# One to four matmuls into unused halves of three PSUM banks, ahead of each tile's product in a gather loop

## The chip, the cores and the metric

The kernel runs on one core of one Trainium2 chip. The metric is the time on the device in microseconds (us), from one launch; smaller is better. The core has the engines TensorE (PE; its weight loads stand in a row of their own, PEld), VectorE (DVE), ScalarE (ACT), GpSimd (POOL) and SyncE (SP), which run side by side and wait for each other by semaphores.

## The reference

The program is one layer of a graph network. The part around the change is the message passing, `agg[dst] += weight * xn[src]` over 100,000 edges and 6,250 nodes of width 256, followed by a linear layer. Beside it run a linear attention and, later, a mixture of eight experts.

```python
def _L0_gnn_ref(x, edge_row, edge_col, edge_val, W, b):
    gathered = edge_val[:, None] * x[edge_col]
    agg = jax.ops.segment_sum(gathered, edge_row, num_segments=N_NODES)
    return jnp.einsum('nd,od->no', agg, W) + b
...
xn = _layernorm(x, axis=-1)
x = x + _L0_gnn_ref(xn, src, dst, edge_weight, L0_gnn_W, L0_gnn_b) + _L0_mix_ref(xn[None], ...)[0]
x = x + _L0_ffn_ref(_layernorm(x, axis=-1)[None], ...)[0]
```

## The kernel before

The edges have been sorted beforehand into tiles of 128 that all end in the same block of 128 nodes; there are 902 such tiles. The linear layer is applied first, so that `z_d` in HBM holds one row per node: a high half and a low half, each 256 numbers of 16 bits. The function `graph` then does five things for each tile t, each on an engine of its own:

- POOL (`gather`, L961) starts an indirect DMA that fetches the 128 rows of `z_d` which the tile's edges name (1 KB each) into one of 12 row buffers (`rows[k]`, k = t mod 12, `UG` = 12). It waits first until the product of 12 tiles earlier is finished (`s_mm[k]`), because that product read the buffer.
- DVE (`compare`, L1067) builds a 0/1 matrix that says which edge goes to which node, six tiles ahead (`LEAD`).
- ACT (`weigh`, L985, twice) multiplies it by the high and the low half of the edge weights into one of eight matrices `hot` (`HG` = 8).
- PE (`product`, L1286 to L1288) multiplies it with the rows in three matmuls of 256 columns, all into columns 0 to 255 of one of three PSUM banks (`out_ps`, `BG` = 3). It waits for `hot`, for the row DMA (`s_row[k]`) and for the add of three tiles earlier (`s_add`), which frees the bank. The last of the three matmuls raises `s_mm[k]`.
- DVE (L1206) waits for `s_mm[k]`, adds the bank to the block of `acc` to which the tile belongs, and raises `s_add[k]`.

Each engine runs its own instructions in the order in which they are written. A turn of the loop (`turn`) does 24 tiles. There are 38 turns, the last of 14 tiles, and other work is written between the tiles: in turns 0 to 12 (312 tiles, called stage 1 here) the keys and values of the attention (`features`), in turns 13 to 26 (336 tiles, stage 2) its queries and output (`attention`), and in turns 27 to 37 (254 tiles, stage 3) in part the splitting of the experts' weights, which needs no PE. The PE work of stages 1 and 2 is in 32-bit numbers (L1222, L1230, L1235, L1257 and so on). `B0` = 13 and `L0` = 27 are the turns at which stages 2 and 3 begin. The gather loop lies between 326 and 1681 us of the span. Before it the edges are sorted, and after it come routing and experts.

Of the kernel before, what the change touches and what calls it, by code (L numbers as in the profile page):

```python
# [11 lines left out]
N, D = 6250, 256  # L12
# [12 lines left out]
UG, HG, OG, BG, LEAD = 12, 8, 4, 3, 6  # L25
# [40 lines left out]
def matrix(a, n, m):  # L66
    return a.rearrange("p (n m) -> p n m", n=n, m=m)
# [30 lines left out]
def build(nc, A, out):  # L98
    ctx = ExitStack()
    with ctx:  # L100
# [38 lines left out]
        with nc.cleanup_on_exit():  # L139
            collect(nc, c)  # L140
        graph(nc, c, A)
        route(nc, c, A)
        experts(nc, c, A)
# [646 lines left out]
def graph(nc, c, A):  # L790
# [8 lines left out]
    hot = [matrix((misc if k < 5 else more).take(2 * P, F16), 2, P) for k in range(HG)]  # L799
# [17 lines left out]
    den, a = big.take(NE), big.take(D)  # L817
# [7 lines left out]
    turns, LOOPS, B0, L0, L1 = ET // UG, ET // (2 * UG), 13, 27, 32  # L825
# [1 line left out]
    assert UG < tiles_of(LOOPS - 1)  # L827
    M2, M9, LAST = 8, 16, 25
    assert 4 * B0 >= NT + 3 and 4 * (L0 - B0) >= NT + 5 and L1 + 5 <= LOOPS and 24 * L1 >= 3 * CW // 2
    out_ps = [c.bank[k][:, 0:D] for k in range(BG)]  # L830
    ctx_ps, tr_ps = matrix(c.bank[3][:, 0:DH * (P + 1)], DH, P + 1), c.bank[3][:, 0:D]
    k_ps, q_ps = [c.bank[4 + u][:, 0:D] for u in range(2)], [matrix(c.bank[4 + u][:, 0:D], DH, P) for u in range(2)]
    v_ps, pj_ps = c.bank[6][:, 0:D], c.bank[7][:, 0:D]
# [5 lines left out]
    s_row, s_mm, s_add = ([S(f"{name}{k}") for k in range(UG)] for name in ("row", "mm", "add"))  # L839
# [15 lines left out]
    def wait(e, sem, n):  # L855

        if not (isinstance(n, int) and n <= 0):
            e.wait_ge(sem, n)
# [25 lines left out]
    with nc.Block(no_gpsimd_drain=True) as block:  # L884
# [331 lines left out]
        def _(e):  # L1216
            def features(j, h, k, s):
                if k == 0 and live(s - 2):
                    e.wait_ge(s_kf, s - 1)
                    e.wait_ge(s_vo, s - 1)  # L1220
                    for m in range(DH):
                        l = e.matmul(ctx_ps[:, m, :], kf[h % 2][:, m * P:m * P + P], vo[h % 2][:, m, :], start=False, stop=False)  # L1222
                    l.then_inc(s_ctx, 1)
                    if isinstance(s, int) and s - 2 == NT - 1:
                        e.matmul(ctx_ps, zeros[:, 0:P], matrix(zeros[:, 0:DH * (P + 1)], DH, P + 1), start=False, stop=True).then_inc(s_ctx, 1)
                if k == 1 and live(s):
                    e.wait_ge(s_x[h], 16 * (j + 1))
                    wait(e, s_kf, s - 1)
                    for x in range(DH):
                        l = e.matmul(k_ps[h % 2], xT[h][:, x, :], wk[:, x, :], start=x == 0, stop=x == 1)  # L1230
                    l.then_inc(s_k, 1)
                if k == 3 and live(s):
                    wait(e, s_vo, s)
                    for x in range(DH):
                        l = e.matmul(v_ps, xT[h][:, x, :], wv[:, x, :], start=x == 0, stop=x == 1)  # L1235
                    l.then_inc(s_vz, 1)

            def attention(j, h, k, b):
                if k == 0 and live(b - 2):
                    if isinstance(b, int) and b == 2:  # L1240
                        e.wait_ge(s_bd, 1)
                    e.wait_ge(s_qf, b - 1)
                    wait(e, s_at, b - 2)
                    for m in range(DH):
                        l = e.matmul(nd_ps[:, m, :], qf[h % 2][:, m, :], sums[:, m, :], start=True, stop=True)
                    l.then_inc(s_nd, 1)
                if k == 1 and live(b):
                    e.wait_ge(s_x[h], 16 * (j - B0 + NT // 4 + (2 if h == 0 else 1)))
                    if isinstance(b, int) and b == 0:
                        e.wait_ge(s_w2, 32)  # L1250
                    if isinstance(b, int) and b < 2:
                        e.wait_ge(s_kf, NT)
                    else:
                        e.wait_ge(s_qf, b - 1)
                    for m in range(DH):
                        for x in range(DH):
                            l = e.matmul(q_ps[h % 2][:, m, :], wq[:, x, m * P:m * P + P], xT[h][:, x, :], start=x == 0, stop=x == 1)  # L1257
                    l.then_inc(s_q, 1)
                if k == 3 and live(b - 2):
                    e.wait_ge(s_at, b - 1)  # L1260
                    wait(e, s_aT, b - 2)
                    for m in range(DH):
                        l = e.transpose(tr_ps[:, m * P:m * P + P], a[:, m * P:m * P + P], c.ident)
                    l.then_inc(s_tr, 1)
                if k == 5 and live(b - 3):
                    e.wait_ge(s_aT, b - 2)
                    wait(e, s_mix, b - 3)
                    for m in range(DH):
                        l = e.matmul(pj_ps, aT[:, m, :], wp[:, m, :], start=m == 0, stop=m == DH - 1)
                    l.then_inc(s_pj, 1)  # L1270

            def scales(h, k):
                if k == 3 and h == 2:
                    e.wait_ge(s_bmax, 1)
                    e.transpose(most_ps[0:2, 0:P], most2[:, 0:2], c.ident).then_inc(s_mt, 1)
                if k == 3 and h == 3:
                    e.wait_ge(s_mr, 1)
                    e.matmul(most_ps[:, 256:260], ones[0:2, :], both[0:2, :], start=True, stop=True).then_inc(s_mb, 1)

            def product(j, t):  # L1280
                q, k = j * 2 + t // UG, t % UG
                e.wait_ge(s_hot, 2 * (j * 2 * UG + t + 1))
                e.wait_ge(s_row[k], 16 * (q + 1))
                wait(e, s_add[(k - BG) % UG], j * 2 + (t - BG) // UG + 1)
                o, w = out_ps[t % BG], hot[t % HG]
                e.matmul(o, w[:, 0, :], rows[k][:, 0:D], start=True, stop=False)  # L1286
                e.matmul(o, w[:, 0, :], rows[k][:, D:2 * D], start=False, stop=False)  # L1287
                e.matmul(o, w[:, 1, :], rows[k][:, 0:D], start=False, stop=True).then_inc(s_mm[k], 1)  # L1288

            def turn(j, at):  # L1290
                for t in range(tiles_of(at)):
                    h = t // 6
                    if at < B0:
                        features(j, h, t % 6, j * 4 + h)
                    elif at < L0:
                        attention(j, h, t % 6, (j - B0) * 4 + h)
                        if at == LAST:
                            scales(h, t % 6)
                    product(j, t)
            e.wait_ge(s_ones, 4)  # L1300
            e.wait_ge(s_w, 16 * 4)
            e.matmul(bias_ps, ones[0:2, :], bias[0:2, :], start=True, stop=True).then_inc(s_bias, 1)
            e.matmul(ctx_ps, zeros[:, 0:P], matrix(zeros[:, 0:DH * (P + 1)], DH, P + 1), start=True, stop=False)
            loops(e, turn)


# [597 lines left out]
```

## Time and profile before

| | |
|---|---|
| median of 3 runs | 2469.26 us (2467.01 to 2470.97) |
| profiled execution, its own time | 2453.38 us |
| its span, first to last instruction | 2451.7 us |
| mean granted TensorE clock, share of full speed | 0.82 |
| PE busy, PE weight loads busy | 1685.1 us (69%), 1215.1 us (50%) |
| DVE, ACT, POOL busy | 1447.4, 1306.2, 1409.0 us |

The page also gives the span in 40 slices of 61 us: a digit is a tenth of the slice, for the engines as busy time and for PEclk as the clock that was granted to TensorE. The gather loop takes slices 6 to 27 or so. A PE at 2.4 GHz all the time would show 9 there. Idle time before an instruction is put down in the views to what ended it. "remote" stands for a semaphore whose raising the profile can't connect with the end of an instruction, and "issue" for nothing that the profile shows.

### The profile page before, as it was taken

How to read it: one execution, taken by the hardware profiler on the slowest of the kernel's cores; microseconds unless marked ns; L12 is line 12 of the kernel's file. 1: busy time of each engine (PE TensorE's matmuls, PEld its weight loads, DVE VectorE, ACT ScalarE, POOL GpSimd, SP SyncE). 2: the span in 40 equal slices, each digit the busy share in tenths (PEclk: the TensorE clock that was granted, in tenths of full speed). 3: DMA queues.
4: the chain of work that ended last, by engine and by line, in shares of the span. 5: the costliest groups of instructions: out<-in, count | busy, mean ns of one | idle time of the engine just before them, and what ended most of it. 6: DMA issues, size and time to landing. Idle time of an engine off the chain costs nothing. (4 is left out here: it accounts for less than half of the span.)

```text
span 2451.7 us, 53365 instructions
## 1 busy us (share of the span) xinstructions
PE 1685.1 (69%) x13546; PEld 1215.1 (50%) x13546; DVE 1447.4 (59%) x3501; ACT 1306.2 (53%) x4202; POOL 1409.0 (57%) x1346
## 2 busy tenths in 40 slices
PE   6776446666666566666664444445379999999998
PEld 3465424444444455555542122213277777777776
DVE  7997535555555565555555555557755555555555
ACT  6454345555555455555555655655306666666665
POOL 3688846666666666666666666665354444444443
PEclk8998768888887787787886565655569999999999
DMA  4022144444444443333333334434302222222222
GB/s 144 18 84 70 54 137 131 131 132 131 129 129 129 132 116 100 100 101 99 100 90 90 91 107 122 151 115 142 109 29 45 47 47 45 47 47 48 46 47 31
DMA packets 140235, 224.43 MB, mean 92 GB/s; under 512 B 34055, under 2 KB 94673, under 8 KB 139955
## 3 DMA queue, kind: packets, MB, share of 16 engines
q0 software_dynamic: 67040, 146.22, 23.2%
q1 hardware_dynamic: 73042, 76.15, 10.2%
q8 instruction: 99, 1.62, 0.3%
q14 instruction: 54, 0.43, 0.1%
HBM read 181.40 MB, written 41.82 MB: 91 GB/s over the span
## 5 line engine op out<-in xcount | busy, mean ns | idle before, releaser
L961 POOL DMA_INDIRECT misc<-z_d,consts x902 | 858.1, 951 | 509.7 <-issue 252.3
L1206 DVE SCALAR_TENSOR_TENSOR acc<-ps,consts,acc 128x256 f32 x902 | 434.3, 482 | 535.7 <-remote 461.1
L1286 PE MATMUL ps<-misc 128*128 128x256 f16 x565 | 186.3, 330 | 309.3 <-DVE acc L1206 150.9
L985 ACT ACTIVATE rec<-rec,misc 128x128 f16<-128x128 f16 x674 | 228.8, 392 | 199.0 <-DVE rec L1067 124.8
L1742 ACT ACTIVATE misc<-ps,misc 128x128 f32<-128x128 f32 x840 | 240.1, 368 | 170.7 <-PE ps L1709 155.4
L1709 PE MATMUL ps<-misc,big 128*128 128x128 f16 x1680 | 327.4, 220 | 0.0
L1707 PE MATMUL ps<-misc,big 128*128 128x128 f16 x1680 | 327.1, 220 | 0.1
L1708 PE MATMUL ps<-misc,big 128*128 128x128 f16 x1680 | 326.9, 220 | 0.0
L1723 PE MATMUL ps<-big,rec 128*128 x840 | 320.2, 382 | 7.3 <-DVE rec L1843 4.9
L985 ACT ACTIVATE misc<-rec,misc 128x128 f16<-128x128 f16 x678 | 228.4, 391 | 145.3 <-DVE rec L1067 114.4
L1775 POOL DMA_INDIRECT misc<-tok_d,pos x105 | 103.8, 988 | 304.0 <-ACT misc L1813 240.5
L1286 PEld LDWEIGHTS ps<-misc 128*128 128x128 f16 x565 | 60.7, 107 | 413.1 <-issue 318.0
L1067 DVE TENSOR_SCALAR rec<-consts,misc 128x128 f16<-128x128 f16 x676 | 186.6, 276 | 59.5 <-issue 57.1
L1841 DVE CAST rec<-misc 128x512 f16<-128x512 f32 x210 | 89.8, 427 | 219.3 <-ACT misc L1742 212.5
L985 ACT ACTIVATE misc<-misc 128x128 f16<-128x128 f16 x452 | 155.9, 392 | 114.4 <-DVE misc L1067 91.9
L1286 PE MATMUL ps<-misc,rec 128*128 128x256 f16 x337 | 112.6, 334 | 141.8 <-issue 78.3
L1707 PEld LDWEIGHTS ps<-misc,big 128*128 x1680 | 164.8, 98 | 88.0 <-issue 1.2
L1782 POOL DMA_INDIRECT out<-misc,pos x105 | 170.5, 1624 | 53.4 <-issue 32.2
L1725 PE MATMUL ps<-big,rec 128*128 x735 | 200.4, 273 | 0.0
L1287 PE MATMUL ps<-misc 128*128 128x256 f16 x565 | 191.5, 339 | 0.0
L1288 PE MATMUL ps<-misc 128*128 128x256 f16 x565 | 191.0, 338 | 0.0
L369 POOL DMA_INDIRECT rec_d<-misc x112 | 155.0, 1384 | 50.1 <-issue 33.8
(335 smaller groups left out, 3884.0 us busy)
## 6 DMA issues: line engine op xcount, KB each, us to landing
big<-in_w2T SPq DMA_DIRECT2D x60, 256.0 KB
misc<-z_d,consts POOLq DMA_INDIRECT x902
big<-xT_d SPq DMA_DIRECT2D x98, 128.0 KB
big<-in_w1T SPq DMA_DIRECT2D x32, 256.0 KB
tok_d<-misc SPq DMA_DIRECT2D x50, 132.0 KB, 1.9
xT_d<-misc SPq DMA_DIRECT2D x49, 128.0 KB
z_d<-misc SPq DMA_DIRECT2D x49, 128.0 KB
acc<-in_x SPq DMA_DIRECT2D x1, 6144.0 KB
```

The lines of the kernel that those rows point to most:

```text
L961: e.indirect_dma_start(out=rows[k], out_offset=None, in_=c.z_d, in_offset=bass.IndirectOffsetOnAxis(ap=idx[u][:, k:k + 1], axis=0)).then_i ...
L985: e.activation(hot[t % HG][:, half, :], same[t % OG], ACT.Copy, scale=near[t // UG][:, t % UG, 1 + half:2 + half]).then_inc(s_hot, 1)
L1206: e.scalar_tensor_tensor(out=rows_of, in0=out_ps[t % BG], scalar=c.gain, in1=rows_of, op0=ALU.mult, op1=ALU.add).then_inc(s_add[k], 1)
L1286: e.matmul(o, w[:, 0, :], rows[k][:, 0:D], start=True, stop=False)
L1287: e.matmul(o, w[:, 0, :], rows[k][:, D:2 * D], start=False, stop=False)
L1288: e.matmul(o, w[:, 1, :], rows[k][:, 0:D], start=False, stop=True).then_inc(s_mm[k], 1)
L1707: e.matmul(o, w1h[:, at], xT[s.u][:, h, :], start=h == 0, stop=False)
L1708: e.matmul(o, w1h[:, at], xT[s.u][:, DH + h, :], start=False, stop=False)
L1709: l = e.matmul(o, w1l[:, at], xT[s.u][:, h, :], start=False, stop=h == DH - 1)
L1723: l = e.matmul(y_ps[s.u], high[s.u][:, m, :], c.w2[:, bass.ds(at, 2 * D)], start=m == 0, stop=m == HB - 1)
L1725: e.matmul(y_ps[s.u][:, 0:D], low[s.u][:, m, :], c.w2[:, bass.ds(at, D)], start=False, stop=False)
L1742: l = e.activation(hidden[:, m, :], h_ps[s.u][:, m, :], ACT.Relu, bias=b1x[s.u][:, m:m + 1])
```

## The change

Each tile's product gets extra matmuls ahead of it: two in stage 1, one in stage 2, four in stage 3. They use the tile's own high `hot` matrix as weights and both halves of `hot` as 256 moving columns. They write columns 256 to 511 of the tile's own bank, which nothing reads. The wait for the bank (`s_add`) is moved ahead of the wait for the rows, and the new matmuls stand between the two. They raise no semaphore. In all they are 2 x 312 + 1 x 336 + 4 x 254 = 1976 matmuls with as many weight loads. No instruction of DVE, ACT, POOL or SP is added or moved.

```diff
-    out_ps = [c.bank[k][:, 0:D] for k in range(BG)]
+    out_ps, unused_ps = ([c.bank[k][:, half * D:half * D + D] for k in range(BG)] for half in range(2))
...
-            def product(j, t):
+            def product(j, t, steady):
                 q, k = j * 2 + t // UG, t % UG
+                o, w = out_ps[t % BG], hot[t % HG]
                 e.wait_ge(s_hot, 2 * (j * 2 * UG + t + 1))
+                wait(e, s_add[(k - BG) % UG], j * 2 + (t - BG) // UG + 1)
+                for _ in range(steady):
+                    e.matmul(unused_ps[t % BG], w[:, 0, :], w.rearrange("p a n -> p (a n)"), start=True, stop=True)
                 e.wait_ge(s_row[k], 16 * (q + 1))
-                wait(e, s_add[(k - BG) % UG], j * 2 + (t - BG) // UG + 1)
-                o, w = out_ps[t % BG], hot[t % HG]
                 e.matmul(o, w[:, 0, :], rows[k][:, 0:D], start=True, stop=False)
...
-                    product(j, t)
+                    product(j, t, 2 if at < B0 else 1 if at < L0 else 4)
```

On PE at the first tiles of stage 1, the difference reads as follows. `ps` is a PSUM bank, `misc` holds `hot` and `rows`, and `big` holds the operands of the attention; x2 are two instructions alike.

```order
-L1302 MATMUL ps<-big 128x256
-L1303 MATMUL ps<-big 128x258
-L1286 MATMUL ps<-misc 128x256
-L1287 MATMUL ps<-misc 128x256
-L1288 MATMUL ps<-misc 128x256
+L1304 MATMUL ps<-big 128x256
+L1305 MATMUL ps<-big 128x258
+L1286 MATMUL ps<-misc 128x256 x2
+L1288 MATMUL ps<-misc 128x256
+L1289 MATMUL ps<-misc 128x256
+L1290 MATMUL ps<-misc 128x256
 L1230 MATMUL ps<-big 128x256 x2
```

Two matmuls now precede the three of the product (which move down by two lines), and the key matmuls of `features` (L1230) follow as they did.

On PE at the first tiles of stage 3, two tiles of before and two of the change:

```order
-L1286 MATMUL ps<-misc 128x256
-L1287 MATMUL ps<-misc 128x256
-L1288 MATMUL ps<-misc 128x256
-L1282 ISA
-L1286 MATMUL ps<-misc 128x256
-L1287 MATMUL ps<-misc 128x256
-L1288 MATMUL ps<-misc 128x256
```

```order
+L1286 MATMUL ps<-misc 128x256 x4
+L1287 ISA
+L1288 MATMUL ps<-misc 128x256
+L1289 MATMUL ps<-misc 128x256
+L1290 MATMUL ps<-misc 128x256
+L1283 ISA
+L1286 MATMUL ps<-misc 128x256 x4
+L1288 MATMUL ps<-misc 128x256
+L1289 MATMUL ps<-misc 128x256
+L1290 MATMUL ps<-misc 128x256
```

A tile of stage 3 has seven matmuls of 256 columns on PE where it had three (ISA rows are waits and register work).

## Rows read from the trace of the kernel before

**Rows 1.** The page, costliest groups: busy and mean ns, then idle before and its releaser.

```profile
L961 POOL DMA_INDIRECT misc<-z_d,consts x902 | 858.1, 951 | 509.7 <-issue 252.3
L1206 DVE SCALAR_TENSOR_TENSOR acc<-ps,consts,acc 128x256 f32 x902 | 434.3, 482 | 535.7 <-remote 461.1
```

**Rows 2.** Windows, one per stage: length, busy us (xcount) by engine, PEclk, DMA, GB/s.

```profile
360.00:794.00 434.00, 275.38 (x1435) 190.08 (x1434) 243.00 (x723) 234.22 (x771) 273.43 (x290) 0.84 0.44 130
794.00:1302.00 508.00, 320.55 (x1902) 246.92 (x1900) 291.02 (x952) 268.91 (x880) 318.75 (x337) 0.82 0.36 104
1302.00:1673.00 371.00, 168.41 (x747) 73.86 (x747) 197.65 (x563) 201.86 (x603) 242.16 (x253) 0.59 0.38 112
```

**Rows 3.** Line L961 from 360 to 1673 us: idle us before it, times, by releaser.

```profile
  issue: 226.3, 713
  remote: 224.7, 138
  PE ps L1288: 27.4, 24
```

**Rows 4.** Timeline of POOL, stage 1: the gathers around one stall.

```profile
746.84 0.94 POOL L961 DMA_INDIRECT misc<-z_d,consts  x1 [0.30 <-issue]
748.08 0.94 POOL L961 DMA_INDIRECT misc<-z_d,consts  x1 [0.30 <-issue]
749.33 0.95 POOL L961 DMA_INDIRECT misc<-z_d,consts  x1 [0.30 <-issue]
752.06 0.94 POOL L961 DMA_INDIRECT misc<-z_d,consts  x1 [1.78 <-remote]
```

**Rows 5.** Timeline of PE, the same stretch.

```profile
745.19 0.27 PE L1286 MATMUL ps<-misc,rec 128*128 128x256 f16 x1
745.29 0.27 PE L1287 MATMUL ps<-misc,rec 128*128 128x256 f16 x1
745.40 0.27 PE L1288 MATMUL ps<-misc,rec 128*128 128x256 f16 x1
...
747.67 0.27 PE L1288 MATMUL ps<-misc 128*128 128x256 f16 x1
752.62 0.37 PE L1286 MATMUL ps<-misc 128*128 128x256 f16 x1 [4.68 <-issue]
```

**Rows 6.** Timeline of DVE, the same stretch.

```profile
746.65 0.25 DVE L1067 TENSOR_SCALAR rec<-consts,misc 128x128 f16<-128x128 f16 x1
751.99 0.48 DVE L1206 SCALAR_TENSOR_TENSOR acc<-ps,consts,acc 128x256 f32 x1 [5.09 <-remote]
...
752.61 0.48 DVE L1206 SCALAR_TENSOR_TENSOR acc<-ps,consts,acc 128x256 f32 x1
```

**Rows 7.** DMA from 747 to 753 us, in 40 slices of 0.15 us.

```profile
GB/s 164 55 137 273 164 246 0 0 0 109 218 218 219 109 0 0 0 0 191 246 137 300 0 0 0 0 164 191 218 246 55 0 0 0 0 0 0 0 0 0
```

**Rows 8.** Timeline of PE, stage 3, at 1.2 GHz, after a stall.

```profile
1524.48 0.42 PE L1288 MATMUL ps<-misc,rec 128*128 128x256 f16 x1
1528.01 0.37 PE L1286 MATMUL ps<-misc 128*128 128x256 f16 x1 [3.11 <-DVE acc L1206]
1528.17 0.42 PE L1287 MATMUL ps<-misc 128*128 128x256 f16 x1
1528.38 0.42 PE L1288 MATMUL ps<-misc 128*128 128x256 f16 x1
```

**Rows 9.** Timeline of DVE, the same stretch.

```profile
1527.38 0.48 DVE L1206 SCALAR_TENSOR_TENSOR acc<-ps,consts,acc 128x256 f32 x1 [3.21 <-remote]
...
1527.99 0.48 DVE L1206 SCALAR_TENSOR_TENSOR acc<-ps,consts,acc 128x256 f32 x1
```

**Rows 10.** Timeline of POOL, the same stretch.

```profile
1524.45 0.95 POOL L961 DMA_INDIRECT misc<-z_d,consts  x1 [0.30 <-issue]
1527.45 0.95 POOL L961 DMA_INDIRECT misc<-z_d,consts  x1 [2.04 <-remote]
```

## The prediction

> **What bounds the kernel now.** I read the page first: its costliest group is the gather on POOL, 902 times, and behind it DVE's add, which idles 461 us for "remote" [rows 1]. Then I read windows by stage. They give the time per tile: 434/290 = 1.50 us in stage 1, 508/337 = 1.51 in stage 2, 371/253 = 1.47 in stage 3 [rows 2]. The reader is to see that the granted clock falls from 0.84 to 0.59 between these stages while the time per tile does not rise. PE's level does not set the pace. No engine is busy for more than two thirds of these windows.
>
> Third, the waits of the gather. A gather takes 0.95 us and the next follows after 0.30 us, so POOL alone needs 1.25 us a tile. The rest comes from 138 + 24 = 162 stalls with 224.7 + 27.4 = 252 us of idle time [rows 3]; less the 0.30 us that would pass anyway, a stall costs 252/162 - 0.30 = 1.26 us. With 878 gathers in that window there is one in 5.4 tiles, and 1.26/5.4 = 0.23 us a tile brings 1.25 to 1.49. So **POOL paces the loop, and what is left over is stalls**, some 200 us over all.
>
> Fourth, the timelines around one stall. POOL's gather at 752.06 waits for the product of 12 tiles earlier [rows 4], which is the one at 745.19 to 745.67 [rows 5]. It should have been free for six microseconds. DVE's add of the same product starts at 751.99 after 5.09 us of "remote" [rows 6]. Both start together, so what came late is PE's semaphore, not a reader. PE meanwhile stands still after 747.67 + 0.27, until DVE has freed a bank. I call this a **held completion**: the matmuls are recorded as done, and their semaphores come up to six microseconds later.
>
> When does the hold end? The traffic shows a burst for each gather, from about 1.6 to 2.3 us after its issue: the issues at 746.84, 748.08 and 749.33 [rows 4] give bursts near 748.4, 749.7 and 750.9, the last over at 751.6 [rows 7]. The hold ends right there, at the adds' 751.99. In stage 3 it is the same: last issue 1524.45, release before the add at 1527.38 [rows 9, 10]. A queue that is full of gathers goes with held completions; POOL then runs out of free buffers, stops, the traffic drains, and the held semaphores arrive. Right after that they are not held: the product at 1528.01 to 1528.80 [rows 8] lets DVE go on.
>
> **How many tiles pass per stall.** From a release on, about 3.0 us are free: POOL issues 0.2 us later, its first burst comes 1.6 us after that, and the second gather's burst, 1.25 us later, finds the queue full again (0.2 + 1.6 + 1.25 = 3.05). In this time pass the three held products (three banks) and those which PE finishes in it. At 1.2 GHz the release is at about 1527.2, the first new product ends at 1528.80, 1.6 us later [rows 8, 9], and the next follow at DVE's spacing of 0.61 us [rows 9]: 1.6, 2.2, 2.8, so three. Six tiles per stall make 1.25 + 1.26/6 = 1.46 us a tile. Stage 3 has 1.47. In stages 1 and 2 the attention's own steps stand between the products and take some of this away.
>
> **What the change adds.** One more matmul of 256 columns takes 0.105 us at 2.4 GHz (745.19, 745.29, 745.40 [rows 5]) and 0.21 us at 1.2 GHz (1528.17 to 1528.38 [rows 8]). The new ones wait for the freed bank as the product does, so they lie wholly between the add and the product of three tiles later. The rows have landed long before (burst over 2.3 us after issue, product some 12 us after), so no wait covers them. During a hold they cost nothing: PE idles then. In the free 3 us they count.
>
> - Stage 3, four, at 1.2 GHz: the first product ends at 1.6 + 0.85 = 2.45, the next at 2.45 + 7 x 0.21 = 3.9. One passes where three did: four per stall, 1.25 + 1.26/4 = 1.565, against 1.46: +0.105 x 254 = **+27 us**. At 2.4 GHz: a product takes 0.48 instead of 0.80, so 1.6 - 0.32 + 0.42 = 1.7, then every 7 x 0.105 = 0.74: 1.7, 2.45, 3.2, so two pass: five per stall, 1.50: **+0.042 x 254 = +11 us**. Seven matmuls per tile are much denser work than three, so the clock should be up more often than the 0.59 of now [rows 2], but each hold leaves PE idle for 4 us and it may fall again. I take the middle, **+18**.
> - Stage 1, two: a clock of 0.84 means 32% of the time at 1.2 GHz. At 2.4 GHz three still pass (1.5, 2.1, 2.7): 0. At 1.2 GHz 2.0, then 3.1: one or two, so 4.5 per stall, +0.07. 312 x 0.32 x 0.07 = **+7**.
> - Stage 2, one: 36% at 1.2 GHz, where 1.8 and then every 0.85 lets two pass, +0.042. 336 x 0.36 x 0.042 = **+5**.
> - Against it: where the new work keeps the clock up, the 32-bit matmuls of stages 1 and 2 run in half the time. I take **-6** for both (half of the two small terms). The lower bound of this credit is nothing. The upper one is what a stage would gain if all its slow time had 2.4 GHz and no new matmuls: 6 tiles would be 6.5 per stall, 0.016 x 648 = 10 us.
>
> Sum: 18 + 7 + 5 - 6 = **+24 us**. The waits for `s_add` and `s_row` only change places: 0. DVE, ACT and SP have no instruction more. The sum is made in the profiled execution (2453.4), which lies 16 us below the median of the runs; added to the median 2469.3 it gives **2493 us**. The case itself spans +6 (the 2.4 GHz values, full credit) to +43 (1.2 GHz throughout stage 3 and 2.5 times the small terms): 2475 to 2512.
>
> **Two rules weighed.** The trace shows both levels, 0.27 and 0.42 us for the same matmul [rows 5, 8], and 0.59 of full speed where PE has only the three. The Trainium skill (TensorE: Matmul & The Clock Gate, "What's actually happening") says that the throttled state is the default and activity releases it. By that rule stage 3 would sit at the 2.4 GHz price, +11 instead of +18, and the sum would be +17; no row here shows seven matmuls per tile.
>
> The trace shows holds that end with the gather traffic. Against my reading stands the Trainium skill (SBUF — State Buffer, "Who interferes with whom"): DMA never contends with a compute engine. If that holds here too, the holds have another cause, and one inside PE could be changed by more PE work. This gives the third rival its weight.
>
> **Rivals.**
> 1. *Nothing changes, 2464 to 2474 us, chance 0.15.* POOL's period is set by its ring of buffers and the drain alone, and PE has slack in the free stretch. For it: the same time per tile at clocks 0.84 and 0.59 [rows 2]. Against it: the third product at 2.8 us has only 0.2 us to spare.
> 2. *PE becomes the bound in stage 3, 2512 to 2545 us, chance 0.12.* If the clock stays at 1.2 GHz, seven matmuls are 7 x 0.21 = 1.49 us a tile, more than POOL's 1.25, and stalls come on top: 1.49 + 0.23 = 1.72 against 1.47, 254 x 0.25 = +64 us at most. It decides when a tile takes PE more than 1.25 us.
> 3. *Faster, 2400 to 2464 us, chance 0.28.* The holds depend on what PE does (its clock, or a next matmul that pushes the last one's completion out), and steady work shortens them or makes them rarer. Each stall less is worth 1.26 us. If a quarter of the 162 go, that is -51 us: about 2418. If all went, -204 us. For it: holds are seen on PE alone, and only when it works in short bursts. Against it: in stage 1 holds of six microseconds come at 2.4 GHz too [rows 5, 6], so the clock is not the cause. It decides once the stalls are fewer than one in 6 tiles.
>
> **Numbers.** The forecast's case has 0.45, the rivals 0.15, 0.12 and 0.28. No difference that can be measured means within 0.2% (5 us), as the runs spread by 2 us to either side. Faster 0.28, same 0.15, slower 0.45 + 0.12 = 0.57. The range leaves out the lower part of rival 3 and the upper part of rival 2, a tenth each: **2425 to 2520 us**; the likeliest case's own range is 2475 to 2512.
>
> **What would show it.** In the profile after, the mean gather stays at 0.95 us and the line "remote" of the gather's waits has more stalls than 138, above all in stage 3: 254/4 to 254/5 = 51 to 64 where there were some 42. The window of stage 3 gets longer by 11 to 27 us, that of stage 2 by less than 6. Its granted clock rises over 0.59. Matmuls ahead of the product follow DVE's add within 0.2 us. The prediction is wrong if the gather's stalls become fewer, or if the gaps between DVE's adds after a release stay at 0.61 us and the number per stall at six.

## The result, and the profile after

The changed kernel takes 2496.92 us (median of 4 runs, 2492.34 to 2497.76), the kernel before 2468.94 (4 runs): a ratio of 1.011, 95% interval 1.0098 to 1.0122. The change costs 28 us. The forecast was 2493. The profiled execution after took 2497.76 us with a span of 2496.0, so it lies at its median, while the one of before was 16 us below its own. The two traces therefore differ by 44 us where the medians differ by 28, and what is read from the pair below has that uncertainty of 16 us.

The page after, the same two groups as [rows 1]:

```profile
L961 POOL DMA_INDIRECT misc<-z_d,consts x902 | 863.5, 957 | 540.3 <-remote 284.0
L1206 DVE SCALAR_TENSOR_TENSOR acc<-ps,consts,acc 128x256 f32 x902 | 434.4, 482 | 574.8 <-remote 495.9
```

The work of both engines is what it was, and the idle time ahead of it grew: by 30.6 us on POOL, by 39.1 us on DVE. The windows of the three stages after, against [rows 2]:

```profile
361.70:802.30 440.60, 317.09 (x2009) 236.30 (x2010) 241.92 (x722) 234.02 (x769) 272.73 (x288) 0.90 0.44 128
802.30:1322.10 519.80, 354.86 (x2237) 276.45 (x2236) 293.05 (x950) 270.43 (x877) 318.44 (x336) 0.85 0.35 102
1322.10:1709.70 387.60, 249.00 (x1748) 182.43 (x1747) 200.41 (x568) 207.71 (x612) 248.56 (x254) 0.87 0.37 108
```

From the first gather of a stage to the first of the next, stage 1 went from 467.6 to 476.2 us, stage 2 from 507.9 to 519.8, and from the first to the last gather of stage 3 from 371.8 to 387.6: +8.6, +11.9, +15.8, which is 36 us in the loop; the other 8 of the 44 lie behind the last gather. The windows leave out the start of stage 1, and their counts of gathers differ from [rows 2] by up to two. The granted clock of stage 3 rose from 0.59 to 0.87.

What the gathers wait for after, from 360 to 1700 us, against [rows 3]:

```profile
  remote: 277.7, 196
  issue: 211.8, 661
  PE ps L1290: 17.2, 14
```

By these labels the stalls went from 162 to 210, and a stall's idle time from 252/162 = 1.56 us to 294.9/210 = 1.40. The labels miss some stalls, which stand under "issue". Counted by the idle time itself (over 0.4 us ahead of a gather, the first gather left out), the whole loop has this:

| gathers that stall, idle us in all | before | after |
|---|---|---|
| stage 1 | 55, 93.4 | 77, 109.0 |
| stage 2 | 84, 112.4 | 81, 123.6 |
| stage 3 | 38, 63.6 | 53, 78.0 |
| loop | 177, 269.3 | 211, 310.6 |

What a stall has beyond the usual 0.30 us adds up to 216 us before and 247 after. These 31 us, and 5 us by which the gathers themselves got longer, are the 36 us of the loop. In stages 1 and 3 there are more stalls and each is shorter; in stage 2 there are not more, and each is longer (1.34 to 1.53 us). A short piece of stage 3 after shows one round. POOL, DVE and the last product ahead of the stall:

```profile
1501.45 0.95 POOL L961 DMA_INDIRECT misc<-z_d,consts  x1 [1.55 <-remote]
1502.70 0.95 POOL L961 DMA_INDIRECT misc<-z_d,consts  x1 [0.30 <-issue]
1503.95 0.94 POOL L961 DMA_INDIRECT misc<-z_d,consts  x1 [0.30 <-issue]
1505.20 0.94 POOL L961 DMA_INDIRECT misc<-z_d,consts  x1 [0.30 <-issue]
1506.45 0.95 POOL L961 DMA_INDIRECT misc<-z_d,consts  x1 [0.30 <-issue]
1508.90 0.95 POOL L961 DMA_INDIRECT misc<-z_d,consts  x1 [1.51 <-remote]
```

```profile
1503.22 0.48 DVE L1206 SCALAR_TENSOR_TENSOR acc<-ps,consts,acc 128x256 f32 x1
1504.55 0.48 DVE L1206 SCALAR_TENSOR_TENSOR acc<-ps,consts,acc 128x256 f32 x1 [0.69 <-PE ps L1290]
...
1508.83 0.48 DVE L1206 SCALAR_TENSOR_TENSOR acc<-ps,consts,acc 128x256 f32 x1 [3.64 <-remote]
```

```profile
1504.18 0.27 PE L1290 MATMUL ps<-misc,rec 128*128 128x256 f16 x1
1504.29 0.60 PE L1286 MATMUL ps<-rec 128*128 128x256 f16 x4
...
1505.83 0.27 PE L1290 MATMUL ps<-misc,rec 128*128 128x256 f16 x1
1509.47 0.80 PE L1286 MATMUL ps<-misc 128*128 128x256 f16 x3 [3.36 <-issue]
```

The reader is to see five gathers from one stall to the next, and the product whose last matmul is recorded from 1504.18 to 1504.45 and whose add comes at 1508.83, 4.4 us later. The holds of before are still there, and in this piece five tiles pass from stall to stall, where the prediction had counted six. From the end of a product to the start of its add the mean went from 3.0 to 2.9 us in stage 1, from 2.3 to 2.3 in stage 2 and from 2.9 to 2.5 in stage 3.

### The profile page after: what moved, and what is told of

It reads as the page before. It is cut to its first block and busy times, and to the rows that moved or that the text cites. A ratio compares the mean times of both kernels' runs of the same rounds, so it can differ in the third digit from the quotient of the medians.

```text
span 2496.0 us, 57314 instructions
## 1 busy us (share of the span) xinstructions
PE 1851.8 (74%) x15522; PEld 1411.0 (57%) x15522; DVE 1448.0 (58%) x3501; ACT 1312.6 (53%) x4202; POOL 1414.3 (57%) x1346
## 5 line engine op out<-in xcount | busy, mean ns | idle before, releaser
L961 POOL DMA_INDIRECT misc<-z_d,consts x902 | 863.5, 957 | 540.3 <-remote 284.0
L1286 PE MATMUL ps<-misc 128*128 128x256 f16 x1240 | 254.7, 298 | 244.5 <-issue 174.0
L1286 PEld LDWEIGHTS ps<-misc 128*128 128x128 f16 x1240 | 117.9, 105 | 326.9 <-issue 256.1
L1286 PE MATMUL ps<-rec 128*128 128x256 f16 x736 | 156.7, 307 | 89.9 <-issue 58.4
L1288 PE MATMUL ps<-misc 128*128 128x256 f16 x565 | 171.4, 303 | 0.6 <-issue 0.6
L1289 PE MATMUL ps<-misc 128*128 128x256 f16 x565 | 170.9, 303 | 0.0
```

The costliest lines, as they stand in the source:

```text
L961: e.indirect_dma_start(out=rows[k], out_offset=None, in_=c.z_d, in_offset=bass.IndirectOffsetOnAxis(ap=idx[u][:, k:k + 1], axis=0)).then_i ...
L1286: e.matmul(unused_ps[t % BG], w[:, 0, :], w.rearrange("p a n -> p (a n)"), start=True, stop=True)
```

## The experiments

The kernels ran in four groups on three chips, each beside the kernel before. There the kernel before took 2222.16, 2222.49, 2221.27 and 2221.77 us, 247 us less than the 2469 of the result. Which chip the result comes from is not on record, so "the chip of the result" below means that chip at that time, and it may be one of these in another condition. None of the experiments' traces shows a held completion. The first question turned from "which part of the change costs 28 us" into "why is it that no part of it costs anything here".

**1. Stage 3's four extra products alone; the ones of stages 1 and 2 alone.** The second has `2 if at < B0 else 1 if at < L0 else 0`.

```
-                    product(j, t, 2 if at < B0 else 1 if at < L0 else 4)
+                    product(j, t, 0 if at < L0 else 4)
```

> Only the four matmuls per tile of stage 3 are kept, none in stages 1 and 2. Theory (the new matmuls lie between DVE's add and the product that waits for it, so fewer tiles pass before completions are held again): +16 us in stage 3 as in the changed kernel's profile, so 2480 to 2488, stalls of the gather in stage 3 about 69 against 42. Rival (the cost comes from stages 1 and 2, where PE is busiest): 2469.

> Only the two and the one matmul of stages 1 and 2 are kept. Theory: the rest of the 28 us, 2480 to 2490 (+9 in stage 1, +12 in stage 2 by the profile of the changed kernel, less what the profile shows over the median). Rival (they are hidden): 2469.

Measured: 2221.84 us, ratio 0.9998 (0.9989 to 1.0007), and 2222.71 us, ratio 0.9998 (0.9989 to 1.0008). Neither part costs anything on this chip. The windows from 325 us by stage of the first:

```profile
325.00:715.00 390.00, 260.04 (x1515) 171.59 (x1515) 268.82 (x784) 258.24 (x831) 293.70 (x310) 0.96 0.54 162
715.00:1136.00 421.00, 296.87 (x1896) 215.43 (x1896) 299.02 (x949) 266.12 (x876) 318.32 (x338) 0.91 0.44 125
1136.00:1456.00 320.00, 235.90 (x1763) 156.74 (x1764) 206.97 (x570) 210.76 (x612) 242.92 (x254) 0.98 0.44 131
```

and stage 3 of the second, where it has no extra product:

```profile
1136.00:1456.00 320.00, 199.37 (x764) 73.53 (x763) 217.12 (x571) 211.69 (x613) 242.85 (x254) 0.51 0.43 130
```

The same 254 gathers in the same 320 us, once at a clock of 0.98 and once at 0.51: 1.26 us a tile, which is the gather's 0.95 and its 0.30. Behind the loop's first gather POOL never stalls. For a loop without stalls this shows what [rows 2] only suggested, that TensorE's level doesn't set the pace.

**2. The extra products off the chain.** Stage 3's four, and none before. They go to bank 4 and stand ahead of the wait for the add, in place of those behind it.

```
+                for _ in range(steady):
+                    e.matmul(c.bank[4][:, 0:D], w[:, 0, :], ..., start=True, stop=True)
                 wait(e, s_add[(k - BG) % UG], j * 2 + (t - BG) // UG + 1)
```

> The four matmuls per tile of stage 3 as in the run of stage 3 alone, but written to a PSUM bank that nothing uses there and put ahead of the wait for the freed bank, so that PE does them while it waits. Theory (the place between add and product costs, the work does not): 2466 to 2474, granted clock in stage 3 about as high as with the change. Rival (more PE work or weight loads cost by themselves): 2480 to 2488, as in the run of stage 3 alone. Rival (a steady clock is worth something once it is off the chain): under 2464.

Measured: 2221.96 us, 1.0001 (0.9993 to 1.001). It tells nothing about the chain, since there was nothing on it to remove.

**3. Six banks for the products of stage 3, no extra product.** The product waits for the add of six tiles earlier. Run twice, the second time beside experiment 6.

```
+    six_ps = [c.bank[k][:, 0:D] for k in (0, 1, 2, 3, 4, 6)]
...
-                o, w = out_ps[t % BG], hot[t % HG]
+                o, w = out_ps[t % BG] if at < L0 else six_ps[t % 6], hot[t % HG]
```

> The kernel before with six PSUM banks for the products of stage 3 instead of three, no new matmuls. Theory (a release lets through what the banks hold plus what is made in the free 3 us: 6 + 3 = 9 tiles per stall instead of 6, so 1.25 + 1.26/9 = 1.39 us a tile against 1.47): 2445 to 2455, stalls of the gather in stage 3 near 28 against 42. Rival (POOL's period is set by its buffers and the drain alone): 2469.

> Stage 3 with six banks for the products in place of four and no extra product. On a chip with holds (before near 2469): if a stall in stage 3 comes because four products' banks are used up while a completion is held, two more banks lengthen the piece between two stalls from 6 tiles to 8, and at 1.26 us a stall stage 3 loses about 11 of its 42 stalls, 13 us: 2455 (2445 to 2465). If the stall comes at its time whatever TensorE still has queued, nothing changes: 2469 (2464 to 2474). On a chip without holds (before near 2222) nothing waits for a bank, and both theories give 2222 within 4.

(The kernel before has three banks there, 0 to 2; the four in the last text is a slip.) Measured: 2221.39 us, 0.9999 (0.999 to 1.0007), and 2223.33 us, 1.001 (1.0001 to 1.002). No wait for a bank, no gain. Whether two more banks lengthen the piece between two stalls is open.

**4. Eight extra products in stage 3.** Experiment 1 with an 8.

> Eight matmuls per tile in stage 3 and none in stages 1 and 2. Theory: the first product after a release ends 0.42 us later than with four at 2.4 GHz and the next 11 x 0.105 = 1.16 us after it, so one passes instead of two, four tiles per stall, 1.565 us a tile: +25 us, 2490 to 2500. Rival (the cost is a fixed one of having extra work): as with four, 2484.

Measured: 2223.14 us, 0.9999 (0.9984 to 1.0013). Eleven matmuls at 0.11 us are 1.2 us a tile, just under POOL's 1.25. PE is busy for 309.61 of the 320 us, and still no gather stalls. The trace has 323.3 us for the stage instead of 320.4, as 14 of its gathers took over 1.1 us themselves.

**5. What the gather costs.** First the landing awaited ahead of the next gather, then the gather replaced by a plain transfer of 128 rows in a row, issued by POOL or by SP with the two queues' roles swapped. The last two read the rows of wrong nodes.

```
+                if k or not first(q):
+                    e.wait_ge(s_row[(k - 1) % UG], 16 * (q + (1 if k else 0)))
```

```
-                e.indirect_dma_start(out=rows[k], out_offset=None, in_=c.z_d, in_offset=...).then_inc(s_row[k], 16)
+                a = (q * UG + k) % NT * P
+                e.dma_start(rows[k], c.z_d[a:a + P, :]).then_inc(s_row[k], 16)
```

> The kernel before, but POOL waits for the landing of one gather before it issues the next, so that bursts never follow each other closely. Theory (completions of PE are held while gathers follow each other in the queue): no holds, DVE's add follows the end of each product within 0.2 us; the loop is paced by 2.4 + 0.1 to 0.2 us a gather, about 3400 to 3500 in all. Rival (holds come from PE itself, which works in short bursts): holds of several microseconds stay, with PE at a still lower clock.

> The indirect gathers are replaced by plain transfers of 128 consecutive rows from POOL's queue, the same bytes (the messages are then those of the wrong nodes). If holds go with POOL's queue whatever its transfers, they stay and the time per tile is 1.25 to 1.5 as the issue of a plain transfer allows. If they go with the indirect form, they vanish and the loop is paced by DVE and PE at 1.0 to 1.25 us a tile, 2100 to 2350 in all.

> The same plain transfers, issued by SP; POOL issues what SP did (blocks of x and weights). If holds go with transfers into SBUF at this rate, they stay. If they go with POOL's queue, they vanish: the loop is then paced by DVE and PE at 1.0 to 1.25 us a tile, 2100 to 2350 in all.

Measured: 4299.76, 1924.41 and 1925.94 us (one run each). All three lie outside what was expected. With one gather in flight a tile takes (4299.76 - 2222.49)/902 = 2.30 us more than 1.25, so 3.55 where about 2.5 was expected. With plain transfers the whole takes 298 us less, whichever queue issues them. None of the three could answer what it was built for, whether holds go with the gathers, since there were no holds to remove. The page of the run with plain transfers on POOL has this:

```profile
L1206 DVE SCALAR_TENSOR_TENSOR acc<-ps,consts,acc 128x256 f32 x902 | 434.4, 482 | 26.7 <-PE ps L1288 8.3
```

DVE idles 26.7 us ahead of its adds where it idled 535.7 in [rows 1]. Without holds POOL's 1.25 us a tile are the bound. DVE, which hardly waits ahead of its adds once the gathers are cheaper, looks like the next one.

**6. The changed kernel itself again.**

> The changed kernel itself, beside the kernel before on one chip. In the profiled pair of the result the 902 products' completions came on average 1.6 to 2.5 us after the recorded end, and the change cost 28 us of 2469 (ratio 1.011). On the two chips of the experiments so far they came 0.014 us after it, the kernel before ran in 2222 us, and every arrangement of the extra products stood within 0.02%. If the cost lies in the held completions, then on a chip with holds (before near 2469) this gives 2497 (2485 to 2510) and 1.011, and on one without (before near 2222) it gives 2222 (2217 to 2228) and a ratio within 0.2% of 1. If instead the whole change, with other counts in each stage than the single parts tried so far, costs what its sum says whatever the chip, it gives 1.011 here too: 2246 beside 2222.

Measured: 2223.26 us (10 runs) beside 2221.27 (19 runs), ratio 1.0008 (0.9999 to 1.0018). The same program costs 1.1% on the chip of the result and nothing that can be told from zero here. What its gathers wait for, from 330 to 1460 us:

```profile
L961 POOL DMA_INDIRECT misc<-z_d,consts x898: 942/946/1449, 329.6 to 1455.8; - x180
its engine sat idle before it (us, times) until:
  issue: 264.4, 868
  PE ps L1290: 9.1, 30
```

No "remote" is left, and 0.30 us passes each time. The timeline of a tile in stage 3:

```profile
1300.04 0.27 PE L1290 MATMUL ps<-misc,rec 128*128 128x256 f16 x1
1300.15 0.60 PE L1286 MATMUL ps<-rec 128*128 128x256 f16 x4
1300.51 0.48 DVE L1206 SCALAR_TENSOR_TENSOR acc<-ps,consts,acc 128x256 f32 x1 [0.23 <-PE ps L1290]
1300.76 0.28 PE L1288 MATMUL ps<-misc,rec 128*128 128x256 f16 x1
```

The add at 1300.51 starts 0.20 us after the recorded end of the last matmul of its product (1300.04 + 0.27); over the whole loop the mean is 0.45, against the 2.3 to 3.0 us of before. On average 2.3 us pass between the add that frees the bank and the product that uses it, and the four extra matmuls fit in them: in stage 3 they end 0.29 us ahead of the product on average, which then waits for the row. From the issue of a gather to the product that uses it 3.1 to 3.4 us pass here, and 12 to 15 in the traces of the result. POOL is far ahead there, so that no wait for a row covers the extra matmuls, as the prediction had it; here PE waits for the rows.

The trace also has the time of each semaphore event. From 800 to 1300 us the events of PE's instructions come 0.014 us after the recorded end here, all 560 of them; in the profiled executions of before and after they come some 1.6 and 1.5 us after it on average (over 400 events each). From 360 to 790 us it is 0.014 against some 2.5 and 2.2. DVE's and ACT's events come 0.01 us after the end in all of them. The two traces of the result lack many of these records: after has 17,433 semaphore events where experiment 6, the same program, has 35,738. So an event can't always be matched with its instruction there, and its averages are rough; the late starts of DVE's adds don't depend on them.

**7. More traffic.** Three more transfers of 256 KB from DRAM to DRAM behind each block of x on SP's queue, in stages 1 and 2.

```
+                wait(e, s_junk, n if n is not None else (s + base) * 48)
+                for x in range(3):
+                    e.dma_start(c.junk_d[x], flat["w2T"][:, part_of(x * CW, CW)]).then_inc(s_junk, 16)
```

> The kernel before with 98 times three more transfers of 256 KB from DRAM to DRAM on SP's queue in stages 1 and 2, 75 MB in all or some 90 GB/s on top of the 100 to 130 of these stages. It asks whether the held completions of the first chip are a matter of how much the transfers carry. If completions are held back by traffic, they are held here too, in stages 1 and 2 alone: gathers stall for over 1.5 us some 50 to 80 times a stage as there, each stall costs 1.26 us, and the time grows by 130 to 200 us (2222 to 2350 or 2420 where the kernel before runs in 2222). If they are something else of that chip, PE's completions stay at 0.014 us, the gather's landings come at most some tenths of a us later, and the time stays within 10 us of before.

Measured: 2221.97 us beside 2221.77, ratio 1.0006 (0.9996 to 1.0016). Its windows of stages 1 and 2:

```profile
325.00:715.00 390.00, 267.86 (x1521) 187.18 (x1521) 264.00 (x774) 254.50 (x831) 295.15 (x312) 0.90 0.84 267
715.00:1136.00 421.00, 294.66 (x1898) 213.02 (x1896) 294.15 (x951) 269.48 (x881) 318.33 (x338) 0.91 0.68 211
```

267 GB/s where experiment 1 has 162, and the 16 engines busy for 0.84 of the time; the gathers keep their pace and PE's events stay at 0.013 us. The rows land later, though: from issue to landing the median in stage 1 is 3.36 us where experiment 1 has 2.68, more than the expected tenths, and it costs nothing. The amount of traffic doesn't make holds on this chip. What it would do on the chip of the result is open. With it stands the Trainium skill (SBUF — State Buffer, "Who interferes with whom"), by which DMA never contends with a compute engine: this trace agrees for PE, with 312 and 338 gathers in the windows in which experiment 1 has 310 and 338, and no late event.

**8. Sixteen extra products in stage 3.** Experiment 1 with a 16.

> Sixteen extra products a tile in stage 3 and none before, where four and eight cost nothing without holds. It sizes the cover: four extra products have to fit in the 2.3 us between the adding of tile n-4 and the landing of tile n's row, and TensorE's own work in the 1.26 us a tile. By the rows at 2.4 GHz an extra product takes about 0.11 us on the engine: 16 of them with the three of the product need 2.0 to 2.1 us a tile, 0.8 us over the pace of the gathers, so stage 3's 254 tiles grow by 190 to 220 us (2222 to 2412 to 2442). If what hides the four is a freer overlap (extra products that cost less than their columns), the time grows by under 100 us. On a chip with holds (before near 2469) TensorE becomes the bound of stage 3 all the same: at 2.05 us a tile against 1.47, 150 us more.

Measured: 2429.49 us beside 2221.77, ratio 1.0937 (1.0919 to 1.0956), +208 us, within the 190 to 220 of the sum. Stage 3 (with the last six gathers of stage 2), and what the gathers of the page wait for:

```profile
1129.00:1642.30 513.30, 509.97 (x4627) 453.35 (x4628) 205.70 (x565) 218.35 (x607) 244.36 (x260) 0.99 0.29 83
```

```profile
L961 POOL DMA_INDIRECT misc<-z_d,consts x902 | 853.6, 946 | 484.1 <-PE ps L1290 261.7
```

PE is busy all the time, 2.0 us a tile, and POOL now waits for products. An extra product costs its 0.11 us once PE is full, and nothing while the sum of PE's work stays under POOL's 1.25 us: eight fit, sixteen don't.

## Why the prediction was right, and where not

The total was right: +24 forecast, +28 measured. That it came so close is in part luck, as its terms were not: in the traces stage 3 grew by 15.8 where the sum had 18, and stages 1 and 2 together by 20.5 where it had 6. Point by point, by its own steps.

**POOL paces the loop, and the rest is stalls.** Right. The 1.25 us floor is what the loop runs at where the stalls are absent. From the first gather to the last it takes 1131 us there (324.5 to 1455.8 in experiment 6) and 1347 here (326.2 to 1673.6), and the difference of 216 us is what the 177 stalls of before add up to beyond their 0.30. Another 12 us lie behind the last add (758 against 770).

**Completions are held.** Confirmed by the comparison: the same program has none of it in the experiments, and the events' own times put the delay on PE alone. That *it has to do with the queue being full of gathers* is not confirmed. The gathers flow at the same rate on chips without holds, experiment 7 adds 105 GB/s without one, and the median time from issue to landing is about the same (2.58 us in stage 1 of before, 2.69 in experiment 6). Nor do all holds end as the prediction read it from two of them. Of the 193 adds of before that waited over 1 us for a product recorded as done, 144 start within 0.7 us of a gather that had stalled; 49 start while POOL keeps its pace and its transfers go on. And a gather stalls because it waits for the same late semaphore, so that the two end together says little of what ends them. PE's events are also late where there is no such gather: by some 0.6 us on average ahead of the loop (0 to 320 us) and 0.4 behind it. The cause of the holds is open.

**Tiles per stall.** The count of gathers per stall was to fall from six to between four and five in stage 3. By the releasers of its gathers stage 3 had 40 stalls in 253 gathers before and 54 in 254 after (51 for "remote", 3 for PE): from 6.3 to 4.7, inside the forecast 51 to 64. By idle time it is 38 and 53 stalls. With the two prices of the prediction and a share of 0.75 of stage 3 at 2.4 GHz, as its trace after has it, the sum gives 0.75 x 11 + 0.25 x 27 = 15 us; 15.8 were measured, but only 9.9 of them are stalls (52.2 to 62.1 us beyond the 0.30), so that this agreement is luck. The price was the term that was off: the sum kept 1.26 us a stall, and it went from 1.37 to 1.17 in this stage. The six tiles are an average, too: in stage 3 of before most stalls stand seven to ten tiles apart and some come two in a row, and after most stand four to six apart. The sign that the extra matmuls follow DVE's add within 0.2 us did come (1508.83 + 0.48, then 1509.47). That the piece is shortened *because the extra products lie between add and product* was argued from timelines and not shown: the experiments made to separate it (2 and 3) ran where there were no stalls.

**A part of stage 3's growth was not on the list.** The idle ahead of its gathers grew by 10 us only (129.1 to 139.3). The gathers themselves grew by 6: 20 of them took over 1.1 us where before 6 did, 8.8 and 2.8 us over the usual 0.95. "The mean gather stays at 0.95 us" failed there (0.98). In experiment 6 it is 6 of them again. In the stage-3 traces of the other experiments it is 3 to 5 without extra products, 8 and 10 with four of them and 14 with eight, so these slow gathers seem to go with the extra work, at 0.4 us or so each; with sixteen, where POOL waits for PE, there are none. Why is open.

**Stages 1 and 2.** The terms +7 and +5 with a credit of -6 measured as +8.6 and +11.9. The clock rose from 0.84 to 0.90 and from 0.82 to 0.85, and nothing that could be called a credit is seen; in a loop without stalls a higher clock gave nothing back at all (experiment 1). Whether the credit was absent or the costs were larger than the terms, this pair can't tell apart. The prediction's bound "stage 2 by less than 6" was wrong, and so was the way: its stalls did not become more frequent (84 and 81) but longer, which the sum with its fixed 1.26 us could not have. In the pair of traces the three stages make 36 where the sum had 24. The medians differ by 28, since the profiled execution of before was itself 16 us under its median.

**The range of the case.** Its ends, +6 and +43, don't come out of the terms as they are told: the 2.4 GHz values with the full credit are 11 - 10 = +1, and 1.2 GHz throughout with 2.5 times the small terms and no credit is 27 + 30 = +57. The measured +28 lies within either.

**The clock.** The prediction took the middle between the two levels, and stage 3 came out at 0.87, nearer to 2.4 GHz. Where PE isn't stopped by holds, the same seven matmuls a tile bring 0.98 and the three alone 0.51. The rule weighed there, of the Trainium skill (TensorE: Matmul & The Clock Gate, "What's actually happening"), that activity releases the throttle, agrees with these rows. The sum by it was +17. The stage's term by it was +11, against 15.8 in all and 9.9 in stalls.

**The rivals.** *Nothing changes* is what the three chips of the experiments show, by another mechanism than the one it named: there are no stalls, and the cover is the 2.3 us in which PE waits for the row. *PE becomes the bound* did not happen with four, and experiment 8 shows where it does. *Faster* fell: stalls became more frequent (177 to 211). They did get shorter on average, from 1.52 to 1.47 us of idle time, most of all in stage 3, so a part of what it said is in the trace, and it was outweighed.

## What to carry to other kernels

Work that is put on an engine that waits is free as long as it ends before what the engine waits for; what decides is the sum of its work against the pace of the engine that bounds (here 1.25 us a tile: eight extra matmuls cost nothing, sixteen cost 208 us). A higher granted clock is worth nothing on an engine that doesn't bound. Before a loss of 1% is put down to a change, see whether the kernel before has waits for "remote" that are absent on another chip: the price of the change may be a price of that chip, or of its condition then. And count stalls by the idle time itself: a label such as "remote" depends on which records the trace has.

## What was not expected of the hardware

- The same kernel took 2469 us in the runs of the result (2467.01 to 2470.97) and 2221 to 2222 in the experiments' (four medians of 80 runs, 2217.5 to 2236.51).
- In the slower case PE's semaphore events come late in the loop, by some 2.2 us on average of nearly 1000, more than 100 of them by over 5 us; in the others they come after 0.014 us. DVE and ACT show nothing of it, and transfers land as fast. Ahead of the gather loop and behind it the delay is there as well but smaller (some 0.6 us from 0 to 320 us, 0.4 from 1900 to 2100). The traces of the slower case also have only half as many semaphore events on record. Nothing in the runs tells where either comes from.
- A plain transfer of 128 rows paces POOL less than an indirect one by enough to take 298 us off the kernel, and it is no matter whether POOL or SP issues it (one run each, 1924.41 and 1925.94 us).
